# One kernel, five stages: transfers, filler work and one copy moved in the stages around self attention

## The reference, cut to what matters

```python
# x (8, 512, 512), ctx (8, 77, 512), cond (8, 512); 16 heads of 32
def layer0(x_q, x_kv, t):
    xq  = ada_ln(x_q, t, Wss_q)                  # (1 + scale) * norm + bias, both from silu(t)
    xkv = ada_ln(x_kv, t, Wss_kv)
    q = heads(xq @ Wq + bq); k, v = heads(xkv @ Wkv + bkv)
    return x_q + (softmax(q k^T / sqrt(32)) v) @ Wp + bp
def layer1(x, c, context):
    shift_a, scale_a, gate_a, shift_m, scale_m, gate_m = silu(c) @ W_mod + b_mod
    q, k, v = heads(modulate(ln(x), shift_a, scale_a) @ W_qkv + b_qkv)
    x = x + gate_a * ((softmax(q k^T * scale) v) @ W_proj + b_proj)       # self attention
    x = x + cross_attention(x -> W_qc, context -> W_kvc) @ W_cproj + b_cproj
    return x + gate_m * mlp(modulate(ln(x), shift_m, scale_m))            # gelu, 512 -> 2048 -> 512
...
```

## Time and profile before

| | |
|---|---|
| time, three runs | 2501.99, 2513.71, 2508.69 us, median 2508.69 |
| the profiled execution | 2510.24 us, span 2508.5 us, 32520 instructions |
| granted TensorE clock, mean | 0.985 of full |
| busy: TensorE, VectorE, ScalarE, GpSimd | 95%, 55%, 40%, 24% of the span |
| transfers | 354.20 MB, mean 141 GB/s |

### The profile page before, as it was taken

The page is one execution under the profiler, slowest core; times in us unless marked ns, Lnnn a source line. Parts: engine busy times, 40 slices in busy tenths (PEclk is TensorE's granted clock), DMA queues, the critical chain, the costliest instruction groups (busy, mean ns, idle before and its releaser), DMA issues.

```text
span 2508.5 us, 32520 instructions
## 1 busy us (share of the span) xinstructions
PE 2386.9 (95%) x12056; PEld 1673.7 (67%) x12056; DVE 1383.5 (55%) x2470; ACT 1011.9 (40%) x1799; POOL 611.2 (24%) x513
## 2 busy tenths in 40 slices
PE   7789999999999999999998889999999999999999
PEld 6656666678776344444444566666688888888887
DVE  5566666744465877777776476666542322222221
ACT  3344544423332655555555244334442332233232
POOL 2102111200001666677666311121211101101100
PEclk9999999999998999999999999999999999999999
DMA  7697787655754555565651687777421101110110
GB/s 238 202 237 207 209 240 207 182 181 184 207 195 148 140 124 134 125 157 134 157 147 57 162 227 190 214 199 206 154 68 59 59 19 42 59 59 1 59 42 17
DMA packets 261324, 354.20 MB, mean 141 GB/s; under 512 B 61027, under 2 KB 109243, under 8 KB 261166
## 3 DMA queue, kind: packets, MB, share of 16 engines
q1 hardware_dynamic: 259998, 348.27, 49.4%
q0 software_dynamic: 1168, 3.85, 0.4%
HBM read 233.78 MB, written 116.69 MB: 140 GB/s over the span
## 4 chain that ended last, share of the span: by engine, by line
PE 79%; DVE 7%; DMA 5%; ACT 4%; issue 3%; SPq 1%; POOL 0%; ACTq 0%; DVEq 0%
PE banks L403 41%; PE banks L2250 14%; PE banks L1948 6%; PE banks L1970 4%; PE banks L1927 4%; PE banks L1990 2%; DMA norm_x<-x 2%; PE banks L1355 2%; PE banks L361 2%; PE banks L1369 2%; PE banks L1376 2%; DVE negated_max L1862 1%; DVE negated_max L1254 1%; DVE norm_stats L319 1%; ACT self_exponentials L2034 1%
## 5 line engine op out<-in xcount | busy, mean ns | idle before, releaser
L2034 ACT ACTIVATE self_exponentials<-banks 128x512 f32<-128x512 f32 x512 | 285.7, 594 | 274.3 <-PE banks L1948 117.4
L1862 DVE TENSOR_REDUCE negated_max<-banks 128x1 f32<-128x512 f32 x512 | 330.0, 676 | 94.3 <-PE banks L1927 93.0
L1827 POOL TENSOR_TENSOR self_exponentials<-self_exponentials,self_exponentials 128x512 f32<-128x512 f32 x252 | 319.8, 1299 | 165.5 <-ACT self_exponentials L2034 165.5
L2250 PE MATMUL banks<-mlp_w_down_hi,out_parts 128*128 128x512 f32 x1024 | 333.8, 389 | 0.1
L344 POOL TENSOR_SCALAR norm_rstd<-norm_mean_var 128x4 f32<-128x4 f32 x32 | 8.1, 252 | 1331.9 <-DVE norm_mean_var L323 1331.9
L2207 DVE TENSOR_TENSOR out_parts<-wide,out_parts 128x512 fp32r<-128x512 f32 x128 | 93.0, 726 | 371.1 <-ACT out_parts L2279 371.1
L2269 ACT ACTIVATE wide<-banks,bias_columns 128x512 f32<-128x512 f32 x128 | 88.3, 690 | 426.0 <-PE banks L403 426.0
L1948 PE MATMUL banks<-self_query_stack,self_key_stack 98*128 98x512 f32 x512 | 233.5, 460 | 9.7 <-ACT self_exponentials L2034 6.8
L1948 PEld LDWEIGHTS banks<-self_query_stack,self_key_stack 98*128 98x128 f32 x512 | 97.1, 191 | 193.8 <-ACT self_exponentials L2034 157.5
L2250 PEld LDWEIGHTS banks<-mlp_w_down_hi,out_parts 128*128 128x128 f32 x1024 | 192.2, 188 | 40.5 <-DVE cross_last_x_rows L1298 0.5
L1927 PE MATMUL banks<-self_key_stack,self_query_stack 96*128 96x512 f32 x512 | 206.1, 406 | 6.8 <-DVE negated_max L1862 6.4
(11 more groups left out here) (208 smaller groups left out, 5282.4 us busy)
## 6 DMA issues: line engine op xcount, KB each, us to landing
...
norm_x<-x SPq DMA_DIRECT2D x24, 1024.0 KB, 8.2
...
x_rows<-x SPq DMA_DIRECT2D x23, 1024.0 KB, 6.0
x<-x_rows SPq DMA_DIRECT2D x22, 1024.0 KB, 5.1
...
```

Of the source, the lines that this page charges most:

```text
L1827: e.tensor_tensor(self.p[kt - 1][:, h, :], self.p[kt - 1][:, h, :], self.p[kt][:, h, :], ALU.add).then_inc(self.paired.sem, 1)
L1862: e.tensor_reduce(k.nm[n % 2][:, h * NT + t:h * NT + t + 1], k.bank[:, self.max_banks.of["max", i], :], AX_X, ALU.max, negate=True).then_i ...
L2034: e.activation(self.p[kt][:, h, :], k.bank[:, self.scores.of["score", i], :], ACT.Exp, scale=SCALE).then_inc(self.exp.sem, 1)
L2250: mm = e.matmul(bank, l, w, start=j == 0 and q == 0, stop=j == JC - 1 and q == 2)
```

## The change

It has six parts.

1. **Preparation.** The context's rstd is one pair of instructions over all five columns, with `mean_var` set to 1.0 by VectorE first; the eleven bias loads are issued before the four weight stages.
2. **Context values held back.** The last two tiles of context values come later among the first attention's steps: behind the first turns of the norm and behind a turn of the maxima, rather than beside its first query products.
3. **Seams of both attentions to the context** (`CrossAttention.run`). In layer 0 the first key stack is loaded right after the key diagonals; in the cross attention after the fourth query, before `fetch(2)`, and there the last quarters of batch 1's norm come one step later and the memsets of `ones` are elsewhere. The norm load of batch 2 is issued ahead of the diagonals of batch 1, and in the loop the next norm load is issued at the end of a batch, ahead of the key stack. The splits of `w_p` go one step later.
4. **Copy of the heads** one turn sooner in `finish` on ScalarE.
5. **Qkv.** Three output tiles from the first batch on; the norm load of the batch after next is issued at the end of a batch (`loading`), ahead of the next store and of self attention's fetches; VectorE's turns of the norm come one product sooner.
6. **Numbers of output tiles** in self attention and the MLP follow from part 5.

The diff, without the lines that only change a size or a count of semaphores:

```diff
--- before.py
+++ after.py
@@ -544,3 +544,3 @@
         yield from braid(some(1, following), some(3, values))
-        yield from braid(some(11, following), after(2, slowly(4, values)))
+        yield from braid(some(15, following), after(8, slowly(3, values)))
 
@@ -569,4 +569,2 @@
                 e.dma_start(self.xc[0:n, t, :], flat[t * P:t * P + n]).then_inc(self.ctx_loaded.sem(t), 16)
-            for p in range(Weights.AHEAD + 1):
-                self.w.stage(e, sp, p)
             for name, n in BIAS_COLS:
@@ -574,2 +572,4 @@
                             k.a[name.replace("_", "_xcond_", 1)][0:n].rearrange("(c p) -> c p", p=P)).then_inc(self.bias_loaded.sem, 16)
+            for p in range(Weights.AHEAD + 1):
+                self.w.stage(e, sp, p)
             load_modulation(0)
@@ -641,8 +641,5 @@
                 pool.wait_ge(*self.s_normed(TT - 1))
-            for w, (r, t0, t1) in enumerate(((P, 0, FULL), (CT - FULL * P, FULL, TT))):
-                e.tensor_scalar(self.rstd[0:r, t0:t1], self.mean_var[0:r, t0:t1, 1], (1e-5, 1e-6)[l], None,
-                                ALU.add).then_inc(self.s_rstd.sem, 1)
-                pool.wait_ge(*self.s_rstd(4 * j + 2 * w))
-                e.tensor_tensor(self.rstd[0:r, t0:t1], self.rstd[0:r, t0:t1], k.minus_half[0:r, 0:t1 - t0],
-                                ALU.pow).then_inc(self.s_rstd.sem, 1)
+            e.tensor_scalar(self.rstd[:], self.mean_var[:, :, 1], (1e-5, 1e-6)[l], None, ALU.add).then_inc(self.s_rstd.sem, 1)
+            pool.wait_ge(*self.s_rstd(2 * j))
+            e.tensor_tensor(self.rstd[:], self.rstd[:], k.minus_half[:], ALU.pow).then_inc(self.s_rstd.sem, 1)
             for _ in range(1 + TT + KC):
@@ -663,2 +660,3 @@
             e.memset(self.cond_T[:], 0.0).then_inc(self.zeroed.sem, 1)
+            e.memset(self.mean_var[:], 1.0).then_inc(self.zeroed.sem, 1)
 
@@ -702,2 +700,3 @@
             dve.wait_ge(*self.s_stats(TT - 1))
+            dve.wait_ge(*self.zeroed(1))
             for t in range(TT):
@@ -709,3 +708,3 @@
             dve.wait_ge(*self.s_aggr(TT - 1))
-            dve.wait_ge(*self.s_rstd(4 * j + 3))
+            dve.wait_ge(*self.s_rstd(2 * j + 1))
             for t in range(TT):
@@ -1028,4 +1027,6 @@
             if g == 0:
-                turning[b] = s.turn(b)
-                return some(1, turning[b])
+                if b not in turning:
+                    turning[b] = s.turn(b)
+                    return some(1, turning[b])
+                return None
             if g == 1:
@@ -1050,3 +1051,3 @@
             yield from braid(s.query(n), quarter(n))
-            if not self.layer:
+            if n == 0 or not self.layer:
                 s.ones(n)
@@ -1054,2 +1055,3 @@
             s.load_diagonals(0)
+            s.load_keys(0)
         yield
@@ -1057,18 +1059,21 @@
         weave(s.fetch(1))
-        yield from braid(s.query(2), s.maxima(0), quarter(2))
-        yield from braid(s.query(3), s.maxima(1), s.max_rows(0), quarter(3))
-        weave(s.fetch(2))
         if self.layer:
-            s.ones(0)
-        s.load_keys(0)
+            yield from braid(s.query(2), s.maxima(0))
+            yield from braid(s.query(3), s.maxima(1), s.max_rows(0), quarter(2))
+            s.load_keys(0)
+        else:
+            yield from braid(s.query(2), s.maxima(0), quarter(2))
+            yield from braid(s.query(3), s.maxima(1), s.max_rows(0), quarter(3))
+        weave(s.fetch(2))
+        yield from braid(s.maxima(2), s.max_rows(1), quarter(3) if self.layer else None)
         s.load_values(0)
-        yield from braid(s.maxima(2), s.max_rows(1))
+        next(quarter(self.LEAD))
         s.load_diagonals(1)
         for n, (b, g) in enumerate(SEQ):
-            if n < G:
-                s.split(self.wp_at + n)
+            if 1 <= n <= G:
+                s.split(self.wp_at + n - 1)
             if g == 0 and b + 1 < B:
-                if self.layer and b == 0:
-                    s.ones(1)
                 s.load_keys(b + 1)
+            if g == 2 and b == 0 and self.layer:
+                s.ones(1)
             if g == 2 and b + 2 < B:
@@ -1097,2 +1102,4 @@
                              s.finish(n - 1) if n else None, quarter(m) if m < LAST and g > 0 else None, *side)
+            if m + 1 < LAST and g == G - 1:
+                next(quarter(m + 1) or iter(()), None)
             if g == 0 and b + 1 < B:
@@ -1442,3 +1449,2 @@
             b, g = SEQ[n]
-            yield
             act.wait_ge(*self.av(n))
@@ -1450,3 +1456,3 @@
             e.copy(k.o_wide[n % 2][:], k.bank[:, self.pairs.of["heads", n], :]).then_inc(self.heads_copied.sem, 1)
-            for _ in range(4):
+            for _ in range(5):
                 yield
@@ -1477,3 +1483,3 @@
 
-    STEPS_AT = {0: 1, 2: 2, 3: 2, 4: 1, 5: 2, 6: 2, 7: 1}
+    STEPS_AT = {1: 2, 2: 2, 3: 1, 4: 2, 5: 2, 7: 1}
 
@@ -1500,3 +1506,3 @@
     def slot(self, i):
-        return i % 2 if i < 2 * G else (i - 2 * G) % 3
+        return i % 3
 
@@ -1513,5 +1519,11 @@
 
+        def loading(b):
+
+            turning = s.turn(b) if b < B else iter(())
+            next(turning, None)
+            return turning
+
         yield from braid(s.turn(0), after(Norm.HEAD, splits()))
+        turning = loading(1)
         for b in range(B):
-            turning = s.turn(b + 1) if b + 1 < B else iter(())
             for m in range(2 * G):
@@ -1534,2 +1546,3 @@
             weave(turning)
+            turning = loading(b + 2)
             if B - 6 < b < B - 3:
@@ -1620,6 +1633,6 @@
             i, col = b * 2 * G + m, BIAS_AT["L1_b_qkv"] + m
-            o, before = (k.two_outs if b == 0 else k.three_outs).take(("qk", i), self.stored(i))
+            o, before = k.three_outs.take(("qk", i), self.stored(i))
             assert o == self.slot(i)
             act.wait_ge(*self.product(i))
-            if i == 2 * G + 2:
+            if i == 2:
                 for done in self.freed_third:
@@ -2115,3 +2128,3 @@
     def hidden_slot(self, i):
-        return (2 * G * (B - 1) + i) % 3
+        return (2 * G * B + i) % 3
 
@@ -2357,3 +2370,3 @@
                       third_out=(l0.based(tiles), prepare.mod_turned(len(SOURCES) - 1), prepare.gates_out(3)))
-        third_out = qkv.stored(2 * G * B - 3)
+        third_out = qkv.stored(2 * G * B - 2)
         attention.set_freed(
```

10 lines of the change are left out of this document (5 added, 5 removed).

## The result

| | before | changed |
|---|---|---|
| median of the runs | 2508.31 us (4) | 2472.42 us (4), 2469.05 to 2475.36 |
| ratio | | 0.9859, 95% interval 0.9839 to 0.9879 |
| the profiled execution | 2510.24 us | 2474.41 us |
| span | 2508.5 us | 2472.6 us |
| TensorE busy, idle | 2386.9, 121.6 us | 2372.6, 100.0 us |

The account below looks back on a forecast made before the run. TensorE, busy 95% of the span, was taken as the bound, so only its idle time or lowered clock could give. Terms of 36.5 us idle and 3.5 us clock, 40.0 off 2510.2, gave 2470.2 us; range 2452 to 2494.

Parts of the forecast that it names:

- Preparation: Before the first attention: one rstd pair and earlier bias loads shorten the wait for normed context, 2 us off.
- First seam: Into the first attention: earlier key stack removes 3.88 us, held-back value tiles give 2.2 us; 6.1 us off together.
- The copy: Both attentions to the context: ScalarE's heads copy one step sooner removes twelve TensorE waits, 9 of 10.7 us credited.
- Three tiles: First batch of qkv: a third output tile ends ScalarE's store wait and TensorE's 3.83 us hole, 3 us off.
- the norm load of qkv: In qkv: norm load issued ahead of stores and fetches ends TensorE's two waits for a norm, 3.4 us off.
- Cross seam: Into the cross attention: 6.2 us of maxima waits go, and less than half of another 6.3; 9 us off.
- Norm loads in the cross attention: Every cross attention batch: norm load ahead of the key stack cuts late maxima, 4 us off.
- The clock: Slices beside the first seam's holes lost 6.9 us to a lowered clock; half, 3.5 us, credited as regained.
- The third one: Rival: 1 MB norm loads delay small loads in both seams, 8.2 us each, 2487 us; counted within next wait's 0.21.
- The second one: Rival: the next wait takes the place of those removed, 25.5 us off, 2485 us; chance 0.21, including delayed small loads.
- The slower one: Rival: denser work in the two attentions makes the clock fall, 2537 us with eight falls; chance 0.04.
- My signs of being right: No hole over 3 us at 115-135 us, no copy waits, VectorE's norm-load waits under 2, cross-seam waits under 5.

Follow-up runs that it names:

- the order most changed: The changed kernel with other places on the queue for diagonals, norm load and first values in both seams: 2472.76 us, ratio 0.9873.

## Why the prediction was right, and where it was not

The time came out at 2472.4 us for 2470 forecast, in the range. The working behind it was right in part, and the number owes something to luck, two errors that cancel: I had expected 36.5 us of idle time and 3.5 us of clock, and the trace shows 21.6 us of idle time and 14.3 of busy time.

**Preparation** (2.0 us credited). The wait for the normed context fell from 12.4 to 10.5 us, and to 9.8 to 11.1 us in the other profiles of the changed kernel and its variants. Right. Some of it was lost within 70 us: the waits for the context's key parts rose from 3.7 to 4.8 us, and the idle time of preparation is 19.8 us in one profile and 17.0 in the other.

**First seam** (6.1). This step failed. The holes of the earlier trace rows went as predicted, but seam and first attention together went only from 34.9 us of idle time to 26.7 and 28.8, and the copy takes 5.0 of that. So 1 to 3 us are left for the loads and the held-back products, and undoing the key stack or the products left the sum where it was (28.3, 27.6). The kernel with the copy alone already has 28.9 us there, and the changed kernel without the earlier norm loads 32.6. So the key stack and the held-back products by themselves did not gain here; if anything they cost, and the norm load made up for it. I named the next wait correctly, the last value tile's store with the diagonals behind it, and gave it to a rival without taking it out of the term: this store kept the diagonals of batch 1 back by 4 us on the queue (130.2 us for 126.0).

**The copy** (9.0). Right, shown twice: 8.9 us of idle time when made alone, 10.7 us of waits when undone. My reason for less than the full 10.7 was later exponentials; what took 2 us back was `sums_turned`. It is the part with the surest cause. Its time was 10 us alone and 12 to 15 when undone; the intervals of the two overlap, and I can't tell them apart.

**Three tiles** (3.0) **and the norm load of qkv** (3.4). 6.4 us credited, 4.4 to 4.7 measured in the stage. The 3.8 us hole fell to 0.9 as predicted, but it is shared by both edits. The norm load alone brings 1.3 us: I had counted VectorE's gain and not the store that was moved back behind the load. I should have priced each transfer that was passed on the queue.

**Cross seam** (9.0). Failed as well: 3.6 us. The maxima behind the memset and split are gone, but 3.9 us for the diagonals came right behind (1420.96 us). That hole lies in the next piece, so the two have to be read together: 34.3 us before, 22.3 and 23.5 in the changed kernel, less 3.9 for the copy, so 7 to 8 us for both this term and the next, which I had put at 13.

**Norm loads in the cross attention** (4.0). The piece went from 23.2 to 14.9 and 15.9 us, 3.9 of it by the copy, so about 4 for the loads even with the new hole in it. Without that hole it would be up to 8, an estimate; with the diagonals ahead of the load the piece has 11.8 us. Undone in both attentions this part costs some 10 to 13 us of idle time. Undersized: by the time (12 to 16 us when undone) it is worth at least as much as the copy.

**The clock** (3.5). Undersized. The loss over slices fell from 37.6 to 25.7 us. A pair of profiles alone would not show that this was earned: in self attention, whose products are the same, the slices lose 11.9 us in the kernel before, 8.5 and 3.4 in the two profiles of the changed kernel, 2.5 to 12.0 in its variants and 1.8 with the copy alone. But every run lists its mean clock. Over 33 runs of the kernel before it is 0.987, over the nine of the changed kernel 0.991, without rounding 0.0045 of some 2500 us, or 11 us, an estimate. With the copy alone it is 0.986, so the gain is not the copy's. Which holes gave it back is not shown. In the stretch that I had named, 120 to 140 us, the changed kernel's slices have 1.00 and 0.88, the second time 1.00 and 0.76, so 1.2 and 2.4 us are lost there for 6.9. But from 60 to 480 us, over the first seam and the first attention, the loss was 8.6 us before and 12.0 and 6.8 in the changed kernel, so falls elsewhere took that place. The Trainium skill (TensorE: Matmul & The Clock Gate, Part 1) has the clock return with sustained work; that agrees with the slices that recovered, and it does not explain slices such as this one of the changed kernel, busy for 9.2 of 10 us, right behind one that was busy for 9.9 at full clock:

```profile
770.00:780.00 10.00, 9.92 (x43) 7.70 (x41) 5.96 (x10) 0.34 (x1) 0.00 (x0) 1.00 0.20 79
780.00:790.00 10.00, 9.22 (x27) 2.68 (x26) 3.21 (x4) 5.68 (x11) 3.71 (x4) 0.66 0.96 231
```

Such a fall stands at this place, the first steps of self attention, in six of the fourteen profiles and in the other eight not.

A small share of the 14.3 us is not the clock. A group of three products of 308 columns lasts 0.69 us right behind a hole and 0.59 where none is (means of 21 and 218 such groups at full clock in the kernel before): compare the rows at 1418.39 above with this one of the kernel before. So each hole removed gives back some 0.1 us more than its idle time, an estimate of 1.7 us for the 17 holes over 0.7 us that the changed kernel has less (34 for 51). That and the 11.9 us of clock nearly make up the 14.3.

```profile
115.38 0.59 PE L403 MATMUL banks<-L_key_diagonals,out_parts 128*128 128x308 f32 x3
```

**The rivals.** The third one, small loads late behind the 1 MB norm loads, came true in both seams, at 3.9 and 2.6 us rather than 8.2 each; in the first seam the store ahead of both had as much part in it. What spoke for it, that order on the queue decides, is only half of it, as three orders gave the same time. The second one, next waits, is the rest of what the seams did not give. The slower one did not happen: no slice of the changed kernel has a clock below 0.66. My signs of being right were met in part: there is no hole over 3 us in 115 to 135 us and the copy is out of the list, but VectorE's waits for the norm load are 3.5 us in qkv (21.2 before) and 4.7 in the cross attention (20.7 before), not under 2, and the waits at the cross seam, with that for the diagonals, still come to some 10 us and not to under 5. Of the signs of being wrong one came true, the hole behind the last value tile's store.

**What stays open.** Why no other order of the loads at the first seam brought the idle time of seam and first attention below the changed kernel's 26.7 and 28.8 us (27.6 with the values back, 27.7 with the diagonals first, 28.3 with the key stack late, 31.4 in the order most changed). The transfer engines' share is 0.81 to 1.13 in the changed kernel's slices from 130 to 180 us, so it may be their capacity; no run took bytes away to show it. No variant beat the changed kernel beyond its interval.
